# Context products with V as the stationary operand, context laid out channels first, expert weights issued later, in a two-layer gated cross-attention kernel

## The chip, the cores and the metric

The kernel runs on one core of one Trainium2 chip. The metric is device time in microseconds (us) of one execution; the time before is the median of three runs.

## The reference

64 batches of 64 rows, 128 channels: x (the query side) and ctx (keys and values) are both [64, 64, 128]. Two layers follow each other, each a gated cross-attention and a gated mixture of experts:

```python
# layer 0 (masked), layer 1 (no mask); H = 16 heads of DK = 8 channels
q = LN(x) @ wq + bq;  k = ctx @ wk + bk;  v = ctx @ wv + bv
scores = where(mask == 0, -1e9, q . k) / sqrt(8)
x = x + tanh(g_xattn[l]) * (softmax(scores) @ v @ wo + bo)
# experts: layer 0 top-1 of 8 (hidden 512, gelu), layer 1 top-2 of 16 with a capacity (hidden 64, silu)
x = x + tanh(g_ffn[l]) * experts_l(LN(x))
```

All of it is float32.

## The kernel before

The 4096 rows are NT = 32 tiles of 128 rows (two batches each), and 8 groups q of Q = 4 tiles (quartets). x stays in SBUF (x_all). Each layer has one `attention` block, in which all engines run at once, and blocks for the experts. In `attention` each engine has a list of steps (function, every, skew): `run` goes through n, and at each n calls, in the list's order, every step whose turn it is; a step with skew s handles tile n - s (or its group, where `every` is 4). So a step with skew -12 works twelve tiles ahead. Each engine executes its instructions in that order, and semaphores tie the engines together.

The path of a tile t of group q, by engine:

- SP (`block.sync`, lines 236 to 250) issues loads, in order, for each q: x(q) (layer 0 only; line 241), ctx(q) (line 244), mask(q) (layer 0; line 247), and at q == 1 the expert weights of the layer (line 250; in layer 0 about 4.6 MB, in layer 1 1.5 MB). x(q) waits for `ln_stats` Q(q-1), ctx(q) for `ctx_turned` q-1, mask(q) for `mask_made` q-1. In layer 1 x is completed by POOL's `fetch` (line 257), an indirect DMA that adds expert outputs into x_all.
- DVE: `stat`, `aggregate` (skew -12, lines 438 to 449) give mean and variance of x; `stat` waits for x(q). `mask` (skew -4, line 461) makes the mask bias. For each tile `maximum` and `subtract` (skew 0, lines 404 to 419) take the row maxima of the two halves of heads and subtract them. `divide` (every 2 tiles, skew 3, line 421) takes reciprocals of the denominators and multiplies. `add` (skew 6) adds the attention output to x, `r_stat`, `r_aggregate` (skew 8) start the second normalization; `choose`, `rows` (skews 18, 19, layer 0) do routing.
- POOL: `norm` (skew -8), `add_bias` (-4), `blocks` (skew -2, line 284), which spreads k into k_blk by heads, `r_norm` (12), the indirect DMAs, and at the start `clear` (line 261), which zeroes v_blk and writes its columns of ones.
- ACT: `normed` (-8) writes the normalized x, and copies PE's results out of PSUM: `ctxT_out`, `xnT_out`, `q_out`, `k_out`, `v_out`, `exp` (which makes probT, keys on partitions), `avT_out`, and `scale_out` (skew 4, layer 0), which scales the expert weights.
- PE: `turn_ctx` (skew -6, line 516) transposes ctx, since rows arrive on partitions; `turn_x` (-5), `project_q` (-4), `project_k` (-3), `project_v` (-2 and -1), `score` (-1, line 574), `turn_probs` (0), `attend` (1, line 603), `turn_av` (3, line 614), `output` (6, line 621), `turn_r`, `logit`, `rank` for routing.

`score` of the next tile needs both `subtract` of this one (`shifted`), since there is one pair of score buffers. In `attend` the probabilities are the stationary operand and V, with a column of ones per head, moves through; rows come out on partitions, 18 columns per pair of heads:

```python
for j in range(HP):
    for b in range(2):
        last = nc.tensor.matmul(AV[b * S:(b + 1) * S, t % 2 * HP + j, :], probT[:, t % 2, j, b * S:(b + 1) * S],
                                v_blk[:, q % 2, u, b, j, :], start=True, stop=True, skip_group_check=True)
```

So the result has to be transposed (`turn_av`, then ACT's `avT_out`) before `output`.

Of the kernel before, what the change touches and what calls it, by code (L numbers as in the profile page):

```python
# [108 lines left out]
def attention(nc, layer, x_all, w, dram, r, hook, sems):  # L109
# [4 lines left out]
    with ExitStack() as ctx:  # L114
# [14 lines left out]
        ctx_in = sb("ctx_in", [P, 2, Q, D])  # L129
# [38 lines left out]
        AV = A_ps[:, 0:2 * HP * VW].rearrange("p (m c) -> p m c", c=VW)  # L168
# [15 lines left out]
        ctx_turned = sem("ctx_turned")  # L184
        ctxT_ready = sem("ctxT_ready")
# [16 lines left out]
        av_turned = sem("av_turned")  # L202
        avT_ready = sem("avT_ready")
# [32 lines left out]
        def _(sp):  # L236
            for q in range(NQ):
# [5 lines left out]
                wait(sp, ctx_turned, q - 1)  # L243
                sp.dma_start(ctx_in[:, q % 2, :, :], dram["ctx"][rows, :].rearrange("(u p) d -> p u d", p=P)).then_inc(ctx_loaded[q % 2], 16)
# [3 lines left out]
                if q == 1:  # L248
                    for to, what, done in hook["experts"]:
                        sp.dma_start(to, what).then_inc(done, 16)  # L250

        @block.gpsimd
        def _(pool):
# [6 lines left out]

            def clear():
                nc.gpsimd.memset(v_blk[:, :, :, :, :, :], 0.0).then_inc(zeroed, 1)
                pool.wait_ge(zeroed, 1)
                for s in range(2):
                    half = slice(s * S, (s + 1) * S)
                    nc.gpsimd.memset(v_blk[half, :, :, :, :, s:s + 1], 1.0).then_inc(zeroed, 1)
                pool.wait_ge(zeroed, 3)
# [45 lines left out]
            if masked:  # L313
                clear()
# [3 lines left out]
            else:  # L318
                for t in range(Q):
                    fetch(t)  # L320
                clear()
                for t in range(Q, 2 * Q):
                    fetch(t)
# [3 lines left out]
        def _(act):  # L327
# [27 lines left out]
            def v_out(h):  # L355
                def step(q):
                    act.wait_ge(v_made, 2 * q + h + 1)
                    act.wait_ge(zeroed, 3)
                    wait(act, av_made, Q * (q - 2) + 2 * h + 2)
                    for s in range(2):  # L360
                        half = slice(s * S, (s + 1) * S)
                        last = nc.scalar.copy(v_blk[half, q % 2, 2 * h:2 * h + 2, :, :, 2 + s * DK:2 + (s + 1) * DK].rearrange("p u b j d -> p (u b j) d"),
                                              V_ps[half, 2 * h:2 * h + 2, :, :, :].rearrange("p u b j d -> p (u b j) d"))
# [33 lines left out]
            steps = [(xnT_out, Q, -4), (r_xnT_out, Q, 17), (ctxT_out, Q, -5), (avT_out, Q, 6), (v_out(0), Q, -1), (v_out(1), Q, 0)]  # L397
# [5 lines left out]
        def _(dve):  # L403
# [17 lines left out]
            def divide(p):  # L421
                dve.wait_ge(av_made, 2 * p + 2)
                nc.vector.reciprocal(rden[:, :, :], AV[:, :, 0:2]).then_inc(rden_ready, 1)
                dve.wait_ge(rden_ready, p + 1)
                wait(dve, av_turned, p - 1)
                h = p % 2
                nc.vector.tensor_tensor(av[:, 2 * h:2 * h + 2, :].rearrange("p u (j r d) -> p (u j) r d", j=HP, r=2),
                                        AV[:, :, 2:].rearrange("p m (r d) -> p m r d", r=2),
                                        rden[:, :, :].unsqueeze(3).to_broadcast([P, 2 * HP, 2, DK]),
# [54 lines left out]
            def rows(q):  # L484
# [7 lines left out]
                for k in range(Q):  # L492
                    if q * Q + k >= RING:
# [4 lines left out]
                     (divide, 2, 3), (add, Q, 6), (stat, 1, -12), (r_stat, 1, 8), (aggregate, 1, -12), (r_aggregate, 1, 8)]  # L498
            if masked:
# [4 lines left out]
        def _(pe):  # L504
            ident = w["ident"]

            def turn_x(q):
                pe.wait_ge(xn_ready, Q * (q + 1))
                pe.wait_ge(ctxT_ready, q + 1)
                if masked:  # L510
                    wait(pe, counted, q - 5)
# [3 lines left out]

            def turn_ctx(q):
                pe.wait_ge(ctx_loaded[q % 2], 16 * (q // 2 + 1))
                wait(pe, xnT_ready, q)
                wait(pe, chosen_ready if masked else logits_read, q - 5)
                for u in range(Q):  # L520
                    last = nc.tensor.transpose(X_ps[:, u, :], ctx_in[:, q % 2, u, :], ident[:, :])
                last.then_inc(ctx_turned, 1)
# [33 lines left out]
            def project_k(q):  # L556
                pe.wait_ge(ctxT_ready, q + 1)
# [45 lines left out]
            def attend(t):  # L603
# [740 lines left out]
```

## Time and profile before

| | |
|---|---|
| median of 3 runs | 700.67 us (699.44 to 700.93) |
| the profiled execution, its own time | 701.08 us |
| its span | 699.3 us |
| mean granted TensorE clock | 0.895 of full |
| PE busy | 545.9 us (78%) |
| DVE, ACT, POOL busy | 411.7, 298.5, 340.6 us |
| L289 POOL, k_blk, 128 times | 139.5 us busy |
| L599 PE, transposes of probabilities | 83.8 us busy |
| L610 PE, `attend`, 2048 records | 72.6 us busy |
| L423 DVE, reciprocals, 32 times | 11.1 us busy |

Layer 0's attention runs from about 10 to 250 us of the span (its last 40 us are the routing's tail), its experts to 352, layer 1's attention from 354 to about 565, the rest to the end. A busy share is an average over these stages, each with its own limit. In a row of the timeline, the number in brackets is the idle time of the engine just before, and behind the arrow what ended it.

### The profile page before, as it was taken

How to read it: one execution, taken by the hardware profiler on the slowest of the kernel's cores; microseconds unless marked ns; L12 is line 12 of the kernel's file. 1: busy time of each engine (PE TensorE's matmuls, PEld its weight loads, DVE VectorE, ACT ScalarE, POOL GpSimd, SP SyncE). 2: the span in 40 equal slices, each digit the busy share in tenths (PEclk: the TensorE clock that was granted, in tenths of full speed). 3: DMA queues.
4: the chain of work that ended last, by engine and by line, in shares of the span. 5: the costliest groups of instructions: out<-in, count | busy, mean ns of one | idle time of the engine just before them, and what ended most of it. 6: DMA issues, size and time to landing. Idle time of an engine off the chain costs nothing. (4 is left out here: it accounts for less than half of the span.)

```text
span 699.3 us, 17278 instructions
## 1 busy us (share of the span) xinstructions
PE 545.9 (78%) x5350; PEld 369.4 (53%) x5351; DVE 411.7 (59%) x1014; ACT 298.5 (43%) x639; POOL 340.6 (49%) x451
## 2 busy tenths in 40 slices
PE   1389999989996408999913689999999744789776
PEld 0145665656665408888801356656666532333665
DVE  3167788888774333444412367877678528831676
ACT  1335666555443103333302455566665421444443
POOL 3355555567544722222268999996664111310221
PEclk9889999999995558999965799999999855999999
DMA  5921101000000121222182111110000000000011
GB/s 159 283 61 40 38 19 40 10 7 11 18 17 15 46 71 51 60 60 61 52 162 31 30 32 32 33 30 3 2 2 2 1 0 0 0 1 0 28 45 49
DMA packets 48478, 28.02 MB, mean 40 GB/s; under 512 B 11936, under 2 KB 45344, under 8 KB 48416
## 3 DMA queue, kind: packets, MB, share of 16 engines
q1 hardware_dynamic: 42064, 22.20, 11.4%
q0 software_dynamic: 5632, 4.20, 3.4%
q10 hardware_dynamic: 720, 0.81, 0.4%
q8 instruction: 38, 0.62, 0.4%
q14 instruction: 24, 0.20, 0.1%
HBM read 19.46 MB, written 7.73 MB: 39 GB/s over the span
## 5 line engine op out<-in xcount | busy, mean ns | idle before, releaser
L289 POOL TENSOR_TENSOR k_blk<-kT,columns 128x512 f32<-128x512 f32 x128 | 139.5, 1176 | 69.1 <-PE S_ps L588 64.1
L408 DVE TENSOR_REDUCE maxes<-S_ps 128x8 f32<-128x512 f32 x128 | 87.6, 684 | 56.2 <-PE S_ps L588 55.9
L371 ACT ACTIVATE probT<-T_ps 128x512 f32<-128x512 f32 x128 | 76.5, 598 | 71.8 <-PE T_ps L599 70.8
L416 DVE TENSOR_TENSOR prob<-S_ps,maxes 128x512 f32<-128x512 f32 x128 | 88.5, 691 | 4.4
L599 PE MATMUL T_ps<-columns,prob 128*128 128x128 f32 x512 | 83.8, 286 | 4.0 <-DVE prob L416 4.0
L599 PEld LDWEIGHTS T_ps<-columns,prob 128*128 128x128 f32 x512 | 55.7, 142 | 57.8 <-issue 50.3
L588 PE MATMUL S_ps<-k_blk,qT 64*64 64x512 f32 x512 | 71.5, 629 | 6.5 <-POOL k_blk L289 6.0
L610 PE MATMUL A_ps<-v_blk,probT 128*64 128x18 f32 x2048 | 72.6, 214 | 0.2
L610 PEld LDWEIGHTS A_ps<-v_blk,probT 128*64 128x64 f32 x2048 | 66.2, 140 | 11.2 <-issue 11.2
L257 POOL DMA_INDIRECT x_all<-expert_out,row_int x32 | 50.7, 1585 | 16.9 <-POOLq L774 10.4
L911 POOL COPY f_w_now<-f_w 128x512 f32 x39 | 24.0, 616 | 71.1 <-PE f_H_ps L950 58.4
L866 DVE TENSOR_TENSOR f_hid<-f_H_ps,f_b 128x512 f32<-128x512 f32 x39 | 27.0, 691 | 40.1 <-PE f_Y_ps L959 31.9
L928 ACT ACTIVATE f_hid<-f_hid 128x512 f32<-128x512 f32 x39 | 24.6, 631 | 52.6 <-DVE f_hid L866 52.6
L332 ACT ACTIVATE xn<-x_all,shift,rstd 128x128 f32<-128x128 f32 x64 | 30.5, 485 | 37.7 <-POOL shift L277 37.6
L444 DVE BATCH_NORM_STATS2 stats<-x_all 128x6 f32<-128x128 f32 x64 | 18.4, 288 | 46.3 <-DMA x_all<-expert_out,row_int 26.8
L950 PE MATMUL f_H_ps<-f_rowsT,f_w_now 128*128 128x128 f32 x312 | 44.7, 288 | 0.7
L1066 POOL COPY c_slots_now<-outT 128x256 f32 (+1 forms) x32 | 13.3, 418 | 63.8 <-POOLq L972 32.8
L959 PE MATMUL f_Y_ps<-f_w,f_hid 128*128 x312 | 42.9, 281 | 0.6 <-ACT f_hid L928 0.4
L950 PEld LDWEIGHTS f_H_ps<-f_rowsT,f_w_now 128*128 128x128 f32 x312 | 39.6, 199 | 4.5 <-issue 4.2
L959 PEld LDWEIGHTS f_Y_ps<-f_w,f_hid 128*128 128x128 f32 x312 | 37.9, 191 | 3.7 <-issue 3.6
L309 POOL DMA_INDIRECT sorted_rows<-r_xn,r_row x32 | 32.0, 1000 | 9.6 <-issue 9.0
L766 PE MATMUL a_X_ps<-a_dispatch,a_xn_now 128*128 128x256 f32 x64 | 24.1, 473 | 11.9 <-DVE a_dispatch L726 11.5
(172 smaller groups left out, 969.4 us busy)
## 6 DMA issues: line engine op xcount, KB each, us to landing
ctx_in<-in_ctx SPq DMA_DIRECT2D x16, 256.0 KB, 3.1
f_rows<-sorted_rows SPq DMA_DIRECT2D x39, 64.0 KB, 1.8
expert_out<-f_done SPq DMA_DIRECT2D x39, 64.0 KB, 1.6
x_all<-in_x SPq DMA_DIRECT2D x8, 256.0 KB, 3.4
f_w<-in_W SPq DMA_DIRECT2D x1, 2048.0 KB, 9.4
out<-c_final SPq DMA_DIRECT2D x32, 64.0 KB, 1.5
mask_in<-in_mask SPq DMA_DIRECT2D x8, 128.0 KB, 2.3
columns<-in_columns ACTq DMA_DIRECT2D x1, 530.0 KB, 5.1
```

The costliest lines, as they stand in the source:

```text
L257: pool.indirect_dma_start(x_all[:, t * D:(t + 1) * D], None, r["expert_out"], bass.IndirectOffsetOnAxis(ap=r["row_int"][:, t:t + 1], axis= ...
L289: last = nc.gpsimd.tensor_tensor(k_blk[:, t % 2, b, :, :], kT[:, q % 2, u, b * S:(b + 1) * S].unsqueeze(1).to_broadcast([P, HP, S]), w["he ...
L309: pool.indirect_dma_start(r["sorted"], bass.IndirectOffsetOnAxis(ap=row[:, t % RING:t % RING + 1], axis=0), r_xn[:, t % RING, :], None).th ...
L332: nc.scalar.activation(xn[:, u, :], x_all[:, t * D:(t + 1) * D], ACT.Identity, bias=shift[:, q % 2, u:u + 1], scale=rstd[:, q % 2, u:u + 1 ...
L371: nc.scalar.activation(probT[:, t % 2, 4 * g:4 * g + 4, :], T_ps[g][:, :, :], ACT.Exp, scale=SCALE).then_inc(probT_ready, 1)
L408: nc.vector.tensor_reduce(maxes[:, t % 2, heads], S_ps[g][:, :, :], X, ALU.max).then_inc(max_ready, 1)
L416: nc.vector.tensor_tensor(prob[:, t % 2, heads, :], S_ps[g][:, :, :], maxes[:, t % 2, heads].unsqueeze(2).to_broadcast([P, HP, S]), ALU.su ...
L588: last = nc.tensor.matmul(S_ps[g][b * S:(b + 1) * S, :, :], qT[rows, q % 2, u, b * S:(b + 1) * S], k_blk[rows, t % 2, b, :, :], start=not ...
L599: last = nc.tensor.transpose(T_ps[g][:, j, :], pair, ident[:, :])
L610: last = nc.tensor.matmul(AV[b * S:(b + 1) * S, t % 2 * HP + j, :], probT[:, t % 2, j, b * S:(b + 1) * S], v_blk[:, q % 2, u, b, j, :], st ...
L950: last = nc.tensor.matmul(H_ps[T.par][:, n, :], w1_now[:, T.par, n * P:(n + 1) * P], rowsT[:, T.par, :], start=True, stop=True)
L959: last = nc.tensor.matmul(Y_ps[T.par][:, 0:D], hid[:, T.par, n, :], w2[:, bass.ds(e, 1), n, :].rearrange("p a c -> p (a c)"), start=n == 0 ...
```

## The change

- ctx is handed over transposed (`ctxT`, channels first) and loaded straight into the ctxT tile. PE's `turn_ctx` and ACT's `ctxT_out` are gone; the load of ctx(q) now waits until V of group q-2 is made, because it writes into the tile that this product reads.
- `attend` has V as the stationary operand, in pieces of 128x32 (four places side by side), and the probabilities move: 16 products with 64 columns, whose results have channels on partitions; and 8 products of 128x32 blocks of ones with 128 columns, which give the denominators, repeated for every channel. `turn_av` and `avT_out` are gone; avT now has two buffers.
- `divide` takes the reciprocal of 256 denominators per partition (before 32) and writes avT.
- v_blk is wider (32 columns per pair), zeroed by DVE at the start of its queue and no longer by POOL.
- The expert weights are issued at q == 3, behind mask(3), instead of q == 1; `scale_out` has skew 16 instead of 4.

```diff
-VW = 2 + 2 * DK
+VW = 4 * DK
...
-                wait(sp, ctx_turned, q - 1)
-                sp.dma_start(ctx_in[:, q % 2, :, :], dram["ctx"][rows, :].rearrange("(u p) d -> p u d", p=P)).then_inc(ctx_loaded[q % 2], 16)
+                wait(sp, v_made, 2 * (q - 1))
+                sp.dma_start(ctxT[:, q % 2, :, :], dram["ctxT"][:, rows].rearrange("d (u p) -> d u p", p=P)).then_inc(ctx_loaded[q % 2], 16)
...
-                if q == 1:
+                if q == 3:
                     for to, what, done in hook["experts"]:
...
             else:
-                for t in range(Q):
-                    fetch(t)
-                clear()
-                for t in range(Q, 2 * Q):
+                for t in range(2 * Q):
                     fetch(t)
...
-            def ctxT_out(q):
-                act.wait_ge(ctx_turned, q + 1)
-                wait(act, v_made, 2 * (q - 1))
-                nc.scalar.copy(ctxT[:, q % 2, :, :], X_ps[:, :, :]).then_inc(ctxT_ready, 1)
...
-            def avT_out(q):
-                act.wait_ge(av_turned, 2 * q + 2)
-                wait(act, y_made, q)
-                nc.scalar.copy(avT[:, :, :], Y_ps[:, :, :]).then_inc(avT_ready, 1)
...
             def divide(p):
+                q, h = p // 2, p % 2
                 dve.wait_ge(av_made, 2 * p + 2)
-                nc.vector.reciprocal(rden[:, :, :], AV[:, :, 0:2]).then_inc(rden_ready, 1)
+                nc.vector.reciprocal(rden[:, :], DEN).then_inc(rden_ready, 1)
                 dve.wait_ge(rden_ready, p + 1)
-                wait(dve, av_turned, p - 1)
-                h = p % 2
-                nc.vector.tensor_tensor(av[:, 2 * h:2 * h + 2, :].rearrange("p u (j r d) -> p (u j) r d", j=HP, r=2),
...
+                wait(dve, y_made, q - 1)
+                nc.vector.tensor_tensor(avT[:, q % 2, 2 * h:2 * h + 2, :].rearrange("p u c -> p (u c)"), AV, rden[:, :],
                                         ALU.mult).then_inc(divided, 1)
...
+            nc.vector.memset(v_blk[:, :, :, :, :, :], 0.0).then_inc(zeroed, 1)
+            nc.vector.memset(ones_blk[:, :], 0.0).then_inc(zeroed, 1)
...
-                for j in range(HP):
-                    for b in range(2):
-                        last = nc.tensor.matmul(AV[b * S:(b + 1) * S, t % 2 * HP + j, :], probT[:, t % 2, j, b * S:(b + 1) * S],
-                                                v_blk[:, q % 2, u, b, j, :], start=True, stop=True, skip_group_check=True)
...
+                for r in range(2):
+                    for j in range(r, HP, 2):
+                        nc.tensor.matmul(DEN[quarter(j), at:at + P], ones_blk[:, (1 - r) * 2 * DK:(3 - r) * 2 * DK], probT[:, t % 2, j, :],
+                                         start=r == 0, stop=r == 1, skip_group_check=True)
+                for b in range(2):
+                    for r in range(2):
+                        for j in range(r, HP, 2):
+                            from_ = v_blk[:, q % 2, u, b, :, :].rearrange("p j c -> p (j c)")[:, j * VW - r * 2 * DK:(j + 1) * VW - r * 2 * DK]
+                            last = nc.tensor.matmul(AV[quarter(j), at + b * S:at + (b + 1) * S], from_, probT[:, t % 2, j, b * S:(b + 1) * S],
+                                                    start=r == 0, stop=r == 1, skip_group_check=True)
...
             def output(q):
-                pe.wait_ge(avT_ready, q + 1)
+                pe.wait_ge(divided, 2 * q + 2)
+                wait(pe, y_added, q)
...
-            attention(nc, 0, x_all, w0, d, r0, {"experts": experts, "act": [(scale_out, 1, 4)]}, sems)
+            attention(nc, 0, x_all, w0, d, r0, {"experts": experts, "act": [(scale_out, 1, 16)]}, sems)
```

How it moves instructions. SP's queue in layer 0 from the second x load on; f_w and f_b are the expert weights and biases. Before:

```order
L241 DMA x_all<-in_x 128x4x128
L244 DMA ctx_in<-in_ctx 128x4x128
L247 DMA mask_in<-in_mask 128x4x64
L250 DMA f_w<-in_W 128x8x512
L250 DMA f_b<-in_b 128x32
L250 DMA f_b<-in_b 128x1024
L250 DMA f_w<-in_W 128x32x128
L241 DMA x_all<-in_x 128x4x128 [waits ln_stats]
L244 DMA ctx_in<-in_ctx 128x4x128 [waits ctx_turned]
L247 DMA mask_in<-in_mask 128x4x64 [waits mask_made]
```

And now, from the fourth ctx load on:

```order
L239 DMA ctxT<-in_ctxT 128x512 [waits v_made]
L242 DMA mask_in<-in_mask 128x4x64 [waits mask_made]
L245 DMA f_w<-in_W 128x8x512
L245 DMA f_b<-in_b 128x32
L245 DMA f_b<-in_b 128x1024
L245 DMA f_w<-in_W 128x32x128
L236 DMA x_all<-in_x 128x4x128 [waits ln_stats]
L239 DMA ctxT<-in_ctxT 128x512 [waits v_made]
```

The four weight loads moved from ahead of x(2) to ahead of x(4), and every ctx load, with mask and the next x behind it, waits for a V product.

PE's queue at the end of a quartet, from `attend` of the tile to the next scores. Before:

```order
L610 MATMUL A_ps<-v_blk,probT 64x18 [waits probT_ready,divided,v_ready]
L610 MATMUL A_ps<-v_blk,probT 64x18 x15
L513 MATMUL X_ps<-columns,xn 128x128 [waits ctxT_ready,xn_ready]
L513 MATMUL X_ps<-columns,xn 128x128 x3
L618 MATMUL Y_ps<-columns,av 128x128 [waits y_added,divided]
L618 MATMUL Y_ps<-columns,av 128x128
L569 MATMUL Q_ps<-columns,ctxT 64x64 [waits v_ready,kT_ready]
L569 MATMUL Q_ps<-columns,ctxT 64x64 x7
```

And now:

```order
L581 MATMUL A_ps<-probT,ones_blk 32x128 [waits probT_ready,zeroed,divided,v_ready]
L581 MATMUL A_ps<-probT,ones_blk 32x128 x7
L587 MATMUL A_ps<-probT,v_blk 32x64 x16
L487 MATMUL X_ps<-columns,xn 128x128 [waits xn_ready]
L487 MATMUL X_ps<-columns,xn 128x128 x3
L534 MATMUL Q_ps<-columns,ctxT 64x64 [waits v_ready,kT_ready]
L534 MATMUL Q_ps<-columns,ctxT 64x64 x7
```

`attend` has 24 products for 16, and the transposes of av between those of x and the V product are gone.

## Rows read from the trace of the kernel before

**Rows 1.** The page, part 2: granted TensorE clock in 40 slices of the span, in tenths.

```profile
PEclk9889999999995558999965799999999855999999
```

**Rows 2.** Busy time by stretch (layer 0, layer 1), columns engine busy (instructions), clock, DMA share, GB/s.

```profile
80.00:100.00 20.00, 19.40 (x244) 11.90 (x240) 16.28 (x40) 12.14 (x24) 9.66 (x12) 1.00 0.12 34
440.00:460.00 20.00, 18.91 (x256) 12.16 (x248) 15.09 (x38) 11.05 (x23) 19.03 (x23) 1.00 0.16 29
```

**Rows 3.** DVE's timeline, layer 0: start us, us, instruction, idle before and releaser.

```profile
79.12 0.69 DVE L408 TENSOR_REDUCE maxes<-S_ps 128x8 f32<-128x512 f32 x1 [0.99 <-PE S_ps L588]
...
81.77 0.28 DVE L444 BATCH_NORM_STATS2 stats<-x_all 128x6 f32<-128x128 f32 x1
...
82.38 1.00 DVE L464 TENSOR_SCALAR mask_zero<-mask_in 128x256 f32<-128x256 int32 x1
...
84.08 0.42 DVE L468 TENSOR_TENSOR mask_bias<-mask_zero,mask_value 128x256 bf16<-128x256 f32 x1
85.67 0.69 DVE L408 TENSOR_REDUCE maxes<-S_ps 128x8 f32<-128x512 f32 x1 [1.17 <-PE S_ps L588]
...
88.32 0.35 DVE L423 RECIPROCAL rden<-A_ps 128x32 f32<-128x32 f32 x1
...
89.05 0.28 DVE L444 BATCH_NORM_STATS2 stats<-x_all 128x6 f32<-128x128 f32 x1
...
90.34 0.69 DVE L408 TENSOR_REDUCE maxes<-S_ps 128x8 f32<-128x512 f32 x1 [0.60 <-PE S_ps L588]
...
95.63 0.69 DVE L408 TENSOR_REDUCE maxes<-S_ps 128x8 f32<-128x512 f32 x1 [0.18 <-PE S_ps L588]
...
100.50 0.69 DVE L408 TENSOR_REDUCE maxes<-S_ps 128x8 f32<-128x512 f32 x1 [0.80 <-PE S_ps L588]
```

**Rows 4.** DVE's timeline, layer 0, once routing runs beside the attention.

```profile
141.16 0.68 DVE L408 TENSOR_REDUCE maxes<-S_ps 128x8 f32<-128x512 f32 x1
...
145.92 0.68 DVE L408 TENSOR_REDUCE maxes<-S_ps 128x8 f32<-128x512 f32 x1
```

**Rows 5.** Groups of DVE instructions: count, then busy us, mean ns, idle before.

```profile
L423 DVE RECIPROCAL rden<-A_ps 128x32 f32<-128x32 f32 x32 | 11.1, 348 | 5.6 <-PE A_ps L610 5.6
...
L490 DVE TENSOR_TENSOR r_picked<-r_place,r_chosen 128x32 f32<-128x32 f32 x8 | 1.5, 194 | 0.0
```

**Rows 6.** PE's timeline around tile 4 of layer 0.

```profile
57.60 0.66 PE L599 MATMUL T_ps<-columns,prob 128*128 128x128 f32 x4
58.19 1.11 PE L610 MATMUL A_ps<-v_blk,probT 128*64 128x18 f32 x32
...
60.04 0.69 PE L569 MATMUL Q_ps<-columns,ctxT 128*64 128x64 f32 x16
```

**Rows 7.** A group of PE's matmuls, 80 to 120 us.

```profile
L588 PE MATMUL S_ps<-k_blk,qT 64*64 64x512 f32 x56 | 7.6, 614 | 0.0
```

**Rows 8.** SP's timeline of DMA issues, layer 0.

```profile
13.10 0.51 SPq L250 DMA_DIRECT2D f_w<-in_W  x1
...
18.07 10.23 SPq L241 DMA_DIRECT2D x_all<-in_x  x1
...
63.56 0.52 SPq L241 DMA_DIRECT2D x_all<-in_x  x1
```

**Rows 9.** All engines' timeline, start of layer 0.

```profile
26.80 4.05 POOL L289 TENSOR_TENSOR k_blk<-kT,columns 128x512 f32<-128x512 f32 x4 [4.91 <-ACT kT L353]
...
32.97 0.30 DVE L444 BATCH_NORM_STATS2 stats<-x_all 128x6 f32<-128x128 f32 x1 [14.17 <-DMA x_all<-in_x]
...
34.92 1.01 PE L582 MATMUL S_ps<-mask_bias,ident_bf 128*128 128x512 bf16 x2 [7.45 <-DVE mask_bias L468]
```

**Rows 10.** The eight x loads of line 241.

```profile
DMA to landing us min/median/max: 2.8/3.4/14.9
```

**Rows 11.** POOL in the timeline at the start of layer 1.

```profile
361.27 2.64 POOL L262 MEMSET v_blk<- 128x2304 f32 x1
...
363.96 0.71 POOL L266 MEMSET v_blk<- 64x128 f32 x2
```

More of the change, by code:

```diff
@@ L259, in fetch @@
                                         compute_op=ALU.add).then_inc(fetched[t % 4], 16)
[L261 to L267, printed above, removed]
             def norm(q):
@@ L361, in step @@
                         half = slice(s * S, (s + 1) * S)
-                        last = nc.scalar.copy(v_blk[half, q % 2, 2 * h:2 * h + 2, :, :, 2 + s * DK:2 + (s + 1) * DK].rearrange("p u b j d -> p (u b j) d"),
+                        last = nc.scalar.copy(v_blk[half, q % 2, 2 * h:2 * h + 2, :, :, s * DK:(s + 1) * DK].rearrange("p u b j d -> p (u b j) d"),
                                               V_ps[half, 2 * h:2 * h + 2, :, :, :].rearrange("p u b j d -> p (u b j) d"))
@@ L498, in _ @@
                      (divide, 2, 3), (add, Q, 6), (stat, 1, -12), (r_stat, 1, 8), (aggregate, 1, -12), (r_aggregate, 1, 8)]
+            nc.vector.memset(v_blk[:, :, :, :, :, :], 0.0).then_inc(zeroed, 1)
+            nc.vector.memset(ones_blk[:, :], 0.0).then_inc(zeroed, 1)
+            dve.wait_ge(zeroed, 2)
+            for s in range(2):
+                nc.vector.memset(ones_blk[s * S:(s + 1) * S, (2 + s) * DK:(3 + s) * DK], 1.0).then_inc(zeroed, 1)
             if masked:
@@ L514, in turn_x @@
                 last.then_inc(x_turned, 1)
[L516 to L522, printed above, removed]
             def turn_r(q):
@@ L607, in attend, with quarter @@
                 pe.wait_ge(probT_ready, 2 * t + 2)
-                for j in range(HP):
-                    for b in range(2):
-                        last = nc.tensor.matmul(AV[b * S:(b + 1) * S, t % 2 * HP + j, :], probT[:, t % 2, j, b * S:(b + 1) * S],
-                                                v_blk[:, q % 2, u, b, j, :], start=True, stop=True, skip_group_check=True)
-                last.then_inc(av_made, 1)
-            def turn_av(p):
-                pe.wait_ge(divided, p + 1)
-                wait(pe, y_added, p // 2)
-                for u in (p % 2 * 2, p % 2 * 2 + 1):
-                    last = nc.tensor.transpose(Y_ps[:, u, :], av[:, u, :], ident[:, :])
-                last.then_inc(av_turned, 1)
+                pe.wait_ge(zeroed, 4)
+                at = t % 2 * P
+                def quarter(j):
+                    return slice(j // 2 * VW, (j // 2 + 1) * VW)
+                for r in range(2):
[8 more added lines that the diff above has]
+                                                    start=r == 0, stop=r == 1, skip_group_check=True)
+                last.then_inc(av_made, 1)
             def output(q):
-                pe.wait_ge(avT_ready, q + 1)
+                pe.wait_ge(divided, 2 * q + 2)
+                wait(pe, y_added, q)
                 for u in range(Q):
-                    last = nc.tensor.matmul(Y_ps[:, u, :], avT[:, u, :], w["wo"][:, :], start=True, stop=True)
+                    last = nc.tensor.matmul(Y_ps[:, u, :], avT[:, q % 2, u, :], w["wo"][:, :], start=True, stop=True)
                 last.then_inc(y_made, 1)
@@ L629, in _ @@
                 steps += [(rank, Q, 19)]
-            run(steps + [(score, 1, -1), (turn_probs(1), 1, 0), (attend, 1, 1), (turn_ctx, Q, -6), (turn_x, Q, -5), (turn_av, 2, 3),
+            run(steps + [(score, 1, -1), (turn_probs(1), 1, 0), (attend, 1, 1), (turn_x, Q, -5),
                          (turn_r, Q, 16), (logit, Q, 17), (project_v(0), Q, -2), (project_v(1), Q, -1)])
@@ L1299 @@
     arrays = {
-        "x": i["x"].reshape(T, D), "ctx": i["ctx_1024"].reshape(T, D), "mask": i["mask_BxSxS2_ik1"].reshape(T, S),
+        "x": i["x"].reshape(T, D), "ctxT": i["ctx_1024"].reshape(T, D).T, "mask": i["mask_BxSxS2_ik1"].reshape(T, S),
     }
```

27 lines of the change are left out of this document (8 added, 19 removed).

## The prediction

> **What bounds it now.** I read the clock by slice first, then busy time by stretch, then DVE's and PE's timelines for one quartet (four tiles, a group q), then SP's queue, because the change moves a wait there. The clock [rows 1] shows 2.4 GHz (a 9) wherever attention runs and 1.2 GHz (a 5) at its start, before it and after it. By stretch [rows 2], PE is busy 19.40 of 20 us in layer 0 and 18.91 in layer 1, where POOL has 19.03: PE sets the pace in layer 0, PE and POOL together in the first half of layer 1 (`fetch` beside `blocks`). DVE has 16.28 and 15.09, so it has about 4 us per 20 in hand.
>
> DVE's timeline [rows 3] gives the pace: the first score reduction of a tile starts at 79.12, 85.67, 90.34, 95.63, 100.50. A quartet takes 21.38 us, as 6.55 + 4.67 + 5.29 + 4.87, and each start waited for PE (brackets). Inside it, the two maxima and two subtractions take 2.65 us (79.12 to 81.77), the normalization statistics 0.61 (81.77 to 82.38), the mask group 2.1 (to 84.50); a `divide` takes 0.73 (88.32 to 89.05), in every second tile. A tile's chain is: scores, 2.65 us of DVE, next scores. DVE's steps behind those 2.65 us are free as long as they fit under the next scores. Once routing runs, one tile of four has no slack: 141.16 to 145.92 without an idle bracket [rows 4].
>
> **The change, part by part.**
>
> *PE in `attend`.* Now 32 records (each f32 matmul leaves two) fill 1.11 us [rows 6]. After: 16 records with 128 columns and 32 with 64. Score products of 512 columns show the rate: eight records, four side by side, in two rounds; 7.6 us for 56 is 1.09 us per eight, less 0.614 for one is 0.48 per round [rows 7], so at most 0.12 for 128 columns, 0.06 for 64. With four column groups side by side each group runs 4 x 0.12 + 8 x 0.06 = 0.96 us. I cost `attend` at no change. Nothing in the trace has four column groups; the other bound is one after the other, 3.8 us.
>
> *PE and ACT copies removed.* Per quartet four ctx transposes (0.59, as the four from 57.60 to 58.19 [rows 6]) and four av transposes in two pairs (about 0.6), so PE's 21.4 falls to 20.2. The two ACT copies lie beside other work.
>
> *DVE's `divide`.* The reciprocal goes from 32 elements per partition to 256. With 32 it takes 348 ns, an ordinary operation on 32 takes 194 [rows 5]. Bounds: the extra is fixed per instruction, then about 0.6 us for 256; or everything scales, 8 x 0.348 = 2.8. I take the ordinary fixed part and let the rest grow: 194 less about 33 for its elements is 0.16 fixed; 0.19 for 32 is 5.9 ns each; 256 give 1.68 us, +1.33 per `divide`. The nearest row is a reciprocal that is already far slower than its element count. A `divide` tile then needs 2.65 + 0.73 + 1.33 + 0.61 = 5.3 us on DVE. Two of the four, 4.67 and 4.87, become 5.3 (+1.1); the others lose PE work and backlog (5.29 to about 4.4, 6.55 to 6.3). First half of layer 0: about zero. Second half: the tile without slack, 4.76, becomes 6.1, and I count +1.3 per quartet, **+5** in four. In layer 1 POOL holds the first half at 19 of 20 us, and the two gains meet the two losses: **-1**.
>
> The Trainium skill (VectorE: DVE Perf Modes, section First, the fixed hardware budget) says that a reciprocal is an iterative divide with a repeat count of 8. An estimate from that page, eight cycles an element at its 0.96 GHz, is 2.1 us for 256 plus some 0.1; the sum would be up to 16 higher. The trace has one size only and fits either.
>
> *SP's queue: ctx.* `ctx(q)` now waits for `v_made` 2(q-1), the V product of group q-2, where it waited for a transpose five steps earlier. SP is in order, so mask(q) and **x(q+1)** stand behind it. V of q-2 is made at the end of PE's step n = 4q-9; DVE needs x(q+1) at step 4q-8, right behind that tile's four score operations. Before, x(5) was issued at 63.56 [rows 8] for a use at 81.77 [rows 3]. After: V runs from 2.4 us after the scores of its tile and takes 0.69 (60.04 against 57.60 [rows 6]); without av transposes and with `attend` already begun I put its end 2.4 us behind DVE's first reduction. Issues of ctx and mask take 0.9, landing 3.4 (median, [rows 10]) to 5 with those two ahead: x lands 6.7 to 8.3 behind, DVE wants it 2.65 behind. Stall about 4.5; the tile takes 2.65 + 4.5 + 0.6 + 2.1 to 3.0 (mask) = about 10.2 against 6.55. For x(5), x(6), x(7): **+11**.
>
> *SP's queue: experts.* Now the 4.6 MB are issued at 13.10, ahead of x(2), which lands at 32.97: 19.9 us later, 14.17 of it a DVE wait [rows 8, 9]. After, they stand behind mask(3) and ahead of x(4). SP gets there when V of group 1 is made, 2.4 + 0.9 us into tile 4; x(4) lands some 19 us behind that (less is ahead of it than before), 22.2 us into the tile, and `stat(16)` wants it at 2.65. DVE stands 19.5 us, and with it everything. The tile takes 2.65 + 19.5 + 0.6 + 2.1 = 24.9 against 6.55: **+18**. PE's clock falls to 1.2 GHz in such a gap, as in the fives of [rows 1]; at the start it took some 5 us of dense work at half speed to return: **+2.5**.
>
> *Start of layer 0.* The first scores waited 7.45 us for a mask that stood behind x(2); k_blk had been begun at 26.80 [rows 9]. Without that wait, and with DVE first clearing v_blk (4096 elements; POOL's 2304 took 2.64 [rows 11]; I take 4 us, which delays statistics by some 1.5), scores come 4.5 earlier. But x(3) now waits for V of group 0 and lands about where it was used before, so the 4.5 goes back: **0**, and with PE idle in between the clock stays low longer, **+1.5**.
>
> *Start of layer 1.* POOL loses 2.64 + 2 x 0.36 of memsets ahead of its norm and blocks [rows 11], which lead to the first scores: **-3.6**. DVE's memset there lies in a wait for x. *Ends of the layers:* transposes and a copy go, the longer reciprocal comes: **-1**.
>
> Sum: 5 - 1 + 11 + 18 + 2.5 + 1.5 + 0 - 3.6 - 1 = +32.4. The profiled execution took 701.08, the median is 700.67: 733.5, or **733** against the median. About 0.2% is what a measurement can tell from no change.
>
> **Rivals.**
> 1. *x is not late* (faster). If the x loads land in time after all, because transfers behind the experts overtake them or V is made much earlier than I place it, the terms 11, 18, 2.5 and 1.5 go and the start keeps its 4.5: 701.1 + 5 - 1 - 4.5 - 3.6 - 1 = 696. It decides once all x waits of layer 0 together are under 5 us. Against it: x(2) behind the same transfers waited 14.17 us. Chance 0.10.
> 2. *Four column groups do not run side by side.* With pairs, as `attend` runs now, the phase takes 2 x 0.96 = 1.9, +0.9 per tile; PE's quartets become 23.8 and 22.4, above DVE's, some +25 in all: 758; one after the other, +2.8 per tile, over 850. The products on 64x64 pieces do run four at a time, though on two row halves. Chance 0.08. The Trainium skill (TensorE: Matmul & The Clock Gate, Measured speedup vs the span model) has 2.38 for three column tiles. An estimate by that share makes the phase 1.2 us and adds under 15 in all; no run here shows it.
> 3. *The reciprocal is short* (0.6 us): `divide` tiles go back to PE's pace, some 14 less: 719. Chance 0.15.
> 4. *The reciprocal is long* (2.8 us): +1.1 for 32 of them, minus what stalls hide, about +30: 763. Chance 0.07.
>
> **Numbers.** The forecast has 0.60; its own range, from a DMA landing 3 us sooner or later and three stalls of 2 to 6 us, is 722 to 747. 708 to 760 leaves out rival 1, the deeper half of rival 2 and half of rival 4, together under 0.2. Faster 0.10 (rival 1), same 0.02, slower 0.88.
>
> **What would show it.** DVE's statistics should wait for x_all some 19 us once near 60 us and about 4.5 us three times (near 100, 120, 140), no wait of 14 us at the start, SP's experts issued near 62 us, a reciprocal of 1.7 us, `attend` near 1.0 us, first scores of layer 1 3 to 4 us sooner after its barrier. The prediction is wrong if no DVE wait on x_all exceeds 5 us, or if `attend` takes over 1.5 us.

## The result, and the profile after

The changed kernel takes 735.89 us (median, 734.41 to 740.64) against 700.8 for the one before: a ratio of 1.0528 (95% interval 1.0477 to 1.0578). The profiled execution spans 733.1 us against 699.3, 33.8 more. The forecast was 733.

The page of the changed kernel: the clock by slice; then groups of instructions (count, then busy us, mean ns of one, idle time before it and what ended it).

```profile
PEclk9989599998999955799995599999999965899999
...
L397 DVE RECIPROCAL rden<-A_ps 128x256 f32<-128x256 f32 x32 | 55.9, 1747 | 3.0 <-PE A_ps L587 3.0
L415 DVE BATCH_NORM_STATS2 stats<-x_all 128x6 f32<-128x128 f32 x64 | 18.4, 288 | 54.5 <-DMA x_all<-in_x 37.5
...
L581 PE MATMUL A_ps<-probT,ones_blk 128*32 128x128 f32 x1024 | 41.9, 281 | 6.3 <-issue 6.3
...
L587 PE MATMUL A_ps<-probT,v_blk 128*32 128x64 f32 x2048 | 43.3, 222 | 0.7 <-issue 0.7
```

Against [rows 1] a 5 has come into the first quarter (the fifth slice, 73 to 92 us). The reciprocal takes 1747 ns where it took 348 [rows 5]. And DVE waits 37.5 us for x, in six places, where the kernel before waits 18.6 us in three, the 14.17 of [rows 9] among them.

DVE's timeline of the changed kernel, from tile 4 of layer 0, the first of its quartet, to tile 9:

```profile
59.37 0.66 DVE L381 TENSOR_REDUCE maxes<-S_ps 128x8 f32<-128x512 f32 x1
...
82.29 0.30 DVE L415 BATCH_NORM_STATS2 stats<-x_all 128x6 f32<-128x128 f32 x1 [20.21 <-DMA x_all<-in_x]
84.02 0.68 DVE L381 TENSOR_REDUCE maxes<-S_ps 128x8 f32<-128x512 f32 x1
...
86.67 1.75 DVE L397 RECIPROCAL rden<-A_ps 128x256 f32<-128x256 f32 x1
...
90.81 0.69 DVE L381 TENSOR_REDUCE maxes<-S_ps 128x8 f32<-128x512 f32 x1 [1.52 <-PE S_ps L553]
...
95.49 0.69 DVE L381 TENSOR_REDUCE maxes<-S_ps 128x8 f32<-128x512 f32 x1 [0.51 <-PE S_ps L553]
...
100.68 0.66 DVE L381 TENSOR_REDUCE maxes<-S_ps 128x8 f32<-128x512 f32 x1
...
107.43 0.29 DVE L415 BATCH_NORM_STATS2 stats<-x_all 128x6 f32<-128x128 f32 x1 [4.05 <-DMA x_all<-in_x]
...
109.81 0.68 DVE L381 TENSOR_REDUCE maxes<-S_ps 128x8 f32<-128x512 f32 x1
```

This is the same view as [rows 3], where a quartet's first reductions stood 6.55, 4.67, 5.29 and 4.87 apart. Here the tile that begins at 59.37 takes 24.65 us, with 20.21 of it a wait for x(4). The next takes 6.79. From 100.68 to 109.81 a quartet's first tile takes 9.13, with 4.05 of it a wait for x(5).

SP's timeline of the changed kernel (start us, us):

```profile
61.63 0.34 SPq L239 DMA_DIRECT2D ctxT<-in_ctxT  x1
62.02 0.43 SPq L242 DMA_DIRECT2D mask_in<-in_mask  x1
62.50 0.51 SPq L245 DMA_DIRECT2D f_w<-in_W  x1
...
64.31 0.86 SPq L245 DMA_DIRECT2D f_w<-in_W  x1
65.21 12.82 SPq L236 DMA_DIRECT2D x_all<-in_x  x1
102.95 0.33 SPq L239 DMA_DIRECT2D ctxT<-in_ctxT  x1
103.33 0.43 SPq L242 DMA_DIRECT2D mask_in<-in_mask  x1
103.80 0.51 SPq L236 DMA_DIRECT2D x_all<-in_x  x1
```

The V product lets the ctx load go 2.26 us behind the tile's first reduction (61.63 against 59.37), the experts go next, and x(4) is issued at 65.21 and used at 82.29: 17.1 us. The issue alone held SP for 12.82, where x(2) behind the same loads took 10.23 [rows 8]. For x(5): released 2.27 behind the reduction (102.95 against 100.68), issued at 103.80, used at 107.43, which is 6.75 behind. The eight x loads together:

```profile
DMA to landing us min/median/max: 2.7/3.6/17.1
```

To see where the 33.8 us come from I cut both profiled spans at the first reduction of a tile (`maximum(0)`) and list each piece beside the recorded terms:

| piece, us | before | after | difference | recorded |
|---|---|---|---|---|
| start to the first reduction of layer 0 | 37.92 | 33.46 | -4.5 | -4.5 |
| tiles 0 to 3 (x(3)) | 19.82 | 25.91 | +6.1 | +4.5 and +1.5 |
| tile 4 (x(4), experts) | 6.55 | 24.65 | +18.1 | +18 |
| the tile behind it (slow clock) | 4.67 | 6.79 | +2.1 | +2.5 |
| tiles 8, 12, 16 (x(5) to x(7)) | 19.65 | 28.41 | +8.8 | +11 |
| rest of layer 0 | 118.6 | 125.5 | +6.9 | +5 |
| last reduction of layer 0 to first of layer 1 | 185.18 | 179.19 | -6.0 | -3.6 and part of -1 |
| layer 1, first reduction to last | 151.99 | 152.64 | +0.7 | -1 |
| from there to the end of the span | 154.9 | 156.6 | +1.6 | part of -1 |

The sum is 33.8. Layer 0 alone holds +42 from its first to its last reduction.

PE's timeline of the changed kernel, one `attend` in layer 0:

```profile
169.06 0.64 PE L581 MATMUL A_ps<-probT,ones_blk 128*32 128x128 f32 x16
169.52 0.63 PE L587 MATMUL A_ps<-probT,v_blk 128*32 128x64 f32 x32
170.08 1.06 PE L504 MATMUL X_ps<-columns,r_xnT 128*128 128x8 f32 x8
```

From its start to that of the next matmuls, 169.06 to 170.08, are 1.02 us. In the kernel before the same stretch for its 32 records (58.19 in [rows 6], to the line below) is 1.04:

```profile
59.23 0.66 PE L513 MATMUL X_ps<-columns,xn 128*128 128x128 f32 x4
```

### The profile page after: what moved, and what is told of

Its sections match the earlier page's. It is cut to its first block and busy times, and to the rows that moved or that the text cites. A ratio compares the mean times of both kernels' runs of the same rounds, so it can differ in the third digit from the quotient of the medians.

```text
span 733.1 us, 19016 instructions
## 1 busy us (share of the span) xinstructions
PE 537.1 (73%) x6246; PEld 351.6 (48%) x6247; DVE 457.7 (62%) x1022; ACT 280.9 (38%) x607; POOL 335.4 (46%) x445
## 5 line engine op out<-in xcount | busy, mean ns | idle before, releaser
L564 PE MATMUL T_ps<-columns,prob 128*128 128x128 f32 x512 | 86.2, 291 | 41.2 <-DVE prob L389 41.0
L553 PE MATMUL S_ps<-k_blk,qT 64*64 64x512 f32 x512 | 75.4, 661 | 8.4 <-POOL k_blk L276 6.4
L397 DVE RECIPROCAL rden<-A_ps 128x256 f32<-128x256 f32 x32 | 55.9, 1747 | 3.0 <-PE A_ps L587 3.0
L415 DVE BATCH_NORM_STATS2 stats<-x_all 128x6 f32<-128x128 f32 x64 | 18.4, 288 | 54.5 <-DMA x_all<-in_x 37.5
L581 PE MATMUL A_ps<-probT,ones_blk 128*32 128x128 f32 x1024 | 41.9, 281 | 6.3 <-issue 6.3
L587 PE MATMUL A_ps<-probT,v_blk 128*32 128x64 f32 x2048 | 43.3, 222 | 0.7 <-issue 0.7
L587 PEld LDWEIGHTS A_ps<-probT,v_blk 128*32 128x32 f32 x2048 | 39.0, 112 | 1.5 <-issue 1.2
```

Of the source, the lines that this page charges most:

```text
L397: nc.vector.reciprocal(rden[:, :], DEN).then_inc(rden_ready, 1)
L553: last = nc.tensor.matmul(S_ps[g][b * S:(b + 1) * S, :, :], qT[rows, q % 2, u, b * S:(b + 1) * S], k_blk[rows, t % 2, b, :, :], start=not ...
L564: last = nc.tensor.transpose(T_ps[g][:, j, :], pair, ident[:, :])
L581: nc.tensor.matmul(DEN[quarter(j), at:at + P], ones_blk[:, (1 - r) * 2 * DK:(3 - r) * 2 * DK], probT[:, t % 2, j, :], start=r == 0, stop=r ...
L587: last = nc.tensor.matmul(AV[quarter(j), at + b * S:at + (b + 1) * S], from_, probT[:, t % 2, j, b * S:(b + 1) * S], start=r == 0, stop=r ...
```

## The experiments

Three things were to be told apart: what the order of SP's loads costs, what the reciprocal costs, and what the new form of `attend` itself is worth. Kernels of one series ran on one chip: runs 1 to 4, then 5, 6, 8 and 9, then 7 and 10. The kernel before had medians of 698.56, 697.16 and 700.31 in the three, and each ratio is against the kernel before on the same chip.

**1. x issued ahead of ctx.** `x_ahead` is the changed kernel with one edit on SP: x(0) and x(1) first, then x(q+1) ahead of ctx(q) and thus ahead of its wait for a V product.

```
-                if masked:
-                    wait(sp, ln_stats, Q * (q - 1))
-                    sp.dma_start(x_all[... q ...]).then_inc(x_in[q % 2], 16)
+                for n in (([0, 1] if q == 0 else [q + 1] if q + 1 < NQ else []) if masked else []):
+                    wait(sp, ln_stats, Q * (n - 1))
+                    sp.dma_start(x_all[... n ...]).then_inc(x_in[n % 2], 16)
```

> The changed kernel, with one thing moved: SP issues x(q+1) ahead of ctx(q) instead of behind mask(q), so no x load stands behind a wait for a V product, and x(4) stands ahead of the expert weights. Theory (the loss is late x loads): the DVE waits on x_all of 3.7, 20.2 and three times 3.4 to 5.4 us go, with the slow clock behind them; 736 falls by some 35 (18.1 + 2.1 for x(4), 8.8 for x(5) to x(7), some 6 at the start) to about 701, between 696 and 706. Rival (the longer reciprocal or the wider attend holds the pace, the waits only show it): it stays above 725.

Measured: 697.83 us, ratio 0.997 (0.9936 to 1.0004). The waits of DVE in this kernel, 9 to 160 us (in total, times, longest):

```profile
DVE maxes L381 <- PE S_ps L553: 15.1, 8, 9.9
...
DVE stats L415 <- DMA x_all<-in_x: 0.3, 1, 0.3
```

Of the 37.5 us of waits for x 0.3 are left, by three lines of SP's program, and with the waits the whole loss is gone. Layer 0 from first to last reduction takes 170.59 us for 211.24 in the changed kernel. Tile by tile, the 40.7 us between them lie in the tiles with a wait for x(3) to x(7) and in the one or two right behind each; every other tile takes the same in both kernels within 0.06 us. x(4) now goes out ahead of ctx(3) and of the experts, and the load behind the experts is x(5), wanted only a quartet later. In the profile of run 8, the same kernel, SP's timeline reads:

```profile
35.53 0.51 SPq L236 DMA_DIRECT2D x_all<-in_x  x1
55.28 0.34 SPq L239 DMA_DIRECT2D ctxT<-in_ctxT  x1
...
58.30 1.26 SPq L245 DMA_DIRECT2D f_w<-in_W  x1
59.60 12.13 SPq L236 DMA_DIRECT2D x_all<-in_x  x1
```

x(4) leaves at 35.53 for 65.21. What the change lost, it lost in the queue that loads x.

**2. Only the experts back.** `experts_back` is the changed kernel with the expert loads ahead of x(2) again.

```
-                if q == 3:
+                if q == 1:
...
-            attention(nc, 0, ..., {"experts": experts, "act": [(scale_out, 1, 16)]}, sems)
+            attention(nc, 0, ..., {"experts": experts, "act": [(scale_out, 1, 4)]}, sems)
```

> The changed kernel with the expert weights issued at q == 1 again (and scale_out at skew 4). Theory: the wait of 20 us at tile 4 becomes one of 3 to 5 like the others, the 14 us wait for x(2) at the start returns: 736 - 20 + 3 + 4.5 is about 723. Rival (the place of the weights does not matter, only the wait for V does): 736.

Measured: 723.85 us, ratio 1.0343 (1.0288 to 1.0397). DVE's timeline of this kernel, its waits for x:

```profile
32.60 0.29 DVE L415 BATCH_NORM_STATS2 stats<-x_all 128x6 f32<-128x128 f32 x1 [13.11 <-DMA x_all<-in_x]
44.08 0.30 DVE L415 BATCH_NORM_STATS2 stats<-x_all 128x6 f32<-128x128 f32 x1 [3.80 <-DMA x_all<-in_x]
70.09 0.30 DVE L415 BATCH_NORM_STATS2 stats<-x_all 128x6 f32<-128x128 f32 x1 [3.91 <-DMA x_all<-in_x]
...
147.03 0.29 DVE L415 BATCH_NORM_STATS2 stats<-x_all 128x6 f32<-128x128 f32 x1 [3.87 <-DMA x_all<-in_x]
```

The 20.21 has become an ordinary wait of 3.91, and 13.11 is back at the start, where attention had not begun. The five waits that are left, 3.80 to 4.06 us each, come from ctx's wait for V alone. So the place of the experts is worth 12 us of the loss (735.89 against 723.85; 13 by the two ratios). The kernel is still 26 us above `x_ahead` (697.83). In the profiled executions ctx's wait accounts for 22 us of that, in layer 0 (192.67 from first to last reduction for 170.59). Another 4 lie before the first reduction (37.54 for 33.42) and belong to the early experts, with their wait of 13.11; the 6.5 between the layers lie for the most part in a stretch that varies (run 10).

**3. The experts late in the kernel before.** `before_experts_late` makes the opposite edit in the kernel before (`q == 3`, `scale_out` at 16), and nothing else.

> The kernel before with only the weights moved to q == 3 (and scale_out at skew 16). Theory: late weights are harmless by themselves, because there SP reaches them at about 39 us and x(4) lands near 58, when it is wanted near 56; the wait of 14 us for x(2) goes and the first scores come about 6 us sooner: 695 to 699. Rival (weights ahead of x(4) cost 18 us wherever SP stands): about 713.

Measured: 697.06 us, ratio 0.9966 (0.9934 to 0.9998). The waits of DVE in this kernel, 9 to 160 us:

```profile
DVE stats L444 <- DMA x_all<-in_x: 7.5, 3, 3.5
```

Without ctx's wait for V, late experts do not hurt: x(4) is issued early enough behind them (at 40.92) that DVE waits 3.46 us there. Layer 0 is 4.8 us longer for it (174.11 for 169.27 from first to last reduction), and the start gains more (the first reduction is at 30.87 for 37.92). So late experts alone cost nothing (-0.3%), the change with early experts, whose loss is the wait for V, costs 3.4% (run 2), and both 5.3%: the same edit is harmless in one kernel and costs 12 us in the other. The experts put some 17 us between issue and landing, and the wait for V puts the issue at the moment of use.

**4. The old `attend` with everything else.** `rows_attend_x_ahead` is `x_ahead` with the products, the reciprocal over 32 elements, the two transposes and the copy of the kernel before, but ctx still loaded channels first. Its diff is the part of the recorded diff on `attend`, `divide`, `turn_av` and `avT_out`, reversed, with GpSimd's `clear` back.

> The kernel before with ctx loaded channels first (no turn_ctx, no ctxT_out), x(q+1) issued ahead of ctx(q), weights at q == 3; attend, divide, turn_av and avT_out as before. Theory (the wide reciprocal takes back what attend's new layout frees, the rest of the change is a gain): 6 us sooner at the start, about 0.5 us of PE per quartet in layer 0 and the second half of layer 1: 688 to 695, below x_ahead. Rival (the new attend is itself a gain): x_ahead is below this one.

Measured: 692.83 us, ratio 0.9928 (0.9895 to 0.9962), 5 us under `x_ahead`. Of the layers the gain is in layer 1: 149.4 us from first to last reduction against 152.7 in `x_ahead`. The first reduction of layer 0 is 1.8 us sooner (31.65 for 33.42), without VectorE's clear of v_blk ahead of the statistics.

**5. A cheap instruction for the reciprocal.** `x_ahead_copy` measures what the long reciprocal costs on the path; it leaves out the division.

```
-                nc.vector.reciprocal(rden[:, :], DEN).then_inc(rden_ready, 1)
+                nc.vector.tensor_copy(rden[:, :], DEN).then_inc(rden_ready, 1)
```

> x_ahead with a plain copy of the 256 denominators where the reciprocal stands, so the attention is multiplied by its denominators, not divided: division is left out. Theory (the 1.75 us reciprocal sets the tiles with a divide, 5.2 to 5.4 us): the copy takes about 0.42, those tiles fall to 4.1 to 4.7 us, 32 of them less what PE then needs: 12 to 20 us below x_ahead, about 682. Rival (PE's wider attend, not the reciprocal, holds those tiles): within 3 us of x_ahead.

Measured: 677.91 us, ratio 0.9729 (0.9693 to 0.9765); 12.6 us under `x_ahead` on the same chip (690.54, run 8). A group of DVE's instructions in this kernel:

```profile
L397 DVE COPY rden<-A_ps 128x256 f32<-128x256 f32 x32 | 13.3, 415 | 1.6 <-PE A_ps L587 1.6
```

DVE is busy 32 x 1.33 = 42.6 us less, and the kernel is 12.6 us shorter. From first to last reduction layer 0 gets 2.8 us shorter (165.98 for 168.81) and layer 1 5.0 (146.75 for 151.78); the stretches behind the layers have 3.2 and 1.9. Most of the 3.2 is in the stretch that varies by 6 us (run 10), so 7.8 us, 18% of the 42.6, are sure to be the reciprocal's, and 12.6, or 30%, only if that stretch is too. The chain that decides is what the prediction said of a `divide` tile: in run 8 such tiles take 5.2 to 5.4 us, here mostly 4.7 in layer 0 and 4.0 to 4.1 in the first half of layer 1. Part of that goes back in the tiles ahead: the first of a quartet in layer 0 takes 6.29 us where it took 5.78 (tile 4).

**6. Column groups one behind the other.** `x_ahead_grouped` changes only the order of the products in `attend`, so that all of one 32-column group stand together.

```
-                for r in range(2):
-                    for j in range(r, HP, 2):
+                for i in range(0, HP, 2):
+                    for r, j in ((0, i), (1, i + 1)):
                         nc.tensor.matmul(DEN[...], ...)
-                for b in range(2):
-                    for r in range(2):
-                        for j in range(r, HP, 2):
+                for i in range(0, HP, 2):
+                    for b in range(2):
+                        for r, j in ((0, i), (1, i + 1)):
                             last = nc.tensor.matmul(AV[...], ...)
```

> x_ahead with the same 24 products in attend in another order: all products of one column group of 32 before the next, instead of the four groups in turn. Theory A (each column group has a queue of its own and runs as soon as its operands are free, whatever the order): attend stays near 1.0 us, time as x_ahead. Theory B (products start in program order, so only neighbours that differ in their column group run side by side): attend takes 2.5 us or more, PE sets the pace of every tile, 750 or above.

Measured: 714.16 us, ratio 1.0255 (1.0218 to 1.0292). Neither theory. PE's timeline of this kernel:

```profile
445.71 0.67 PE L581 MATMUL A_ps<-probT,ones_blk 128*32 128x128 f32 x16
446.17 1.37 PE L587 MATMUL A_ps<-probT,v_blk 128*32 128x64 f32 x32
447.47 0.66 PE L564 MATMUL T_ps<-columns,prob 128*128 128x128 f32 x4
```

The products with ones, four records in a row for each group, take what they took, but the AV products, eight in a row, take 1.37 us for 0.63. `attend` is 1.76 us long (445.71 to 447.47), and the kernel 23.6 us longer than `x_ahead` on the same chip. So the four groups do run side by side in the order of `x_ahead`, and an order in the program can take that away.

**7. Four records in a row for AV.** `x_ahead_grouped_av4` leaves the products with ones as in `x_ahead` and puts `for i` inside `for b`, so that four AV records of a group stand in a row.

```
                 for b in range(2):
-                    for r in range(2):
-                        for j in range(r, HP, 2):
+                    for i in range(0, HP, 2):
+                        for r, j in ((0, i), (1, i + 1)):
```

> x_ahead with only the AV products reordered: one column group's two products (four records) one behind the other before the next group's, for each half of the tile; the products with ones stay as in x_ahead. In x_ahead_grouped four records in a row left the products with ones as they were (0.67 us) and eight in a row made the AV products 1.37 us instead of 0.63. If what decides is how many records of one group stand in a row, the AV products here take 0.63 to 0.75 us and the time equals x_ahead (690 to 698 us, -1 to 0%). If what decides is the number of columns between two groups or something in the AV products themselves, they take 1.0 us or more and the time is 12 us or more above it.

Measured: 698.43 us, ratio 0.9977 (0.9946 to 1.0007), as `x_ahead`. PE's timeline of this kernel:

```profile
454.32 0.64 PE L581 MATMUL A_ps<-probT,ones_blk 128*32 128x128 f32 x16
454.78 0.68 PE L587 MATMUL A_ps<-probT,v_blk 128*32 128x64 f32 x32
455.39 0.66 PE L564 MATMUL T_ps<-columns,prob 128*128 128x128 f32 x4
```

Four in a row cost almost nothing (0.68 us), eight double the phase. Eight records of 64 columns and four of 128 are the same number of columns, and only the first is slow. That points to the number of records in a row and not of columns. It isn't shown for both kinds of products: eight in a row were tried for the AV products alone. What in TensorE sets that number stays open.

**8. `x_ahead` again.** The same kernel as in run 1, on the chip of runs 5, 6 and 9.

> x_ahead once more, on the chip of these runs, for the comparison with its two variants and with the kernel before: 0.3% below the kernel before, as in the first series, interval from -0.6% to 0.

Measured: 690.54 us (688.92 to 691.43), ratio 0.9915 (0.9886 to 0.9944), outside what was expected. Why is open. Cut as in the table of the result, the profiled execution of run 1 is longer by 1.8 us in layer 0, 0.9 in layer 1 and 1.3 behind it, and shorter by 1.2 between the layers.

**9. Layer 1's clear on VectorE, old `attend`.** `rows_attend_clear_dve` is run 4 with GpSimd's clear of v_blk in layer 1 moved to VectorE.

```
             def clear():
+                if not masked:
+                    return
...
+            else:
+                nc.vector.memset(v_blk[:, :, :, :, :, :], 0.0).then_inc(zeroed, 1)
+                dve.wait_ge(zeroed, 1)
+                for s in range(2):
+                    nc.vector.memset(v_blk[s * S:(s + 1) * S, :, :, :, :, s:s + 1], 1.0).then_inc(zeroed, 1)
```

> rows_attend_x_ahead with v_blk of layer 1 cleared by DVE instead of POOL, ahead of DVE's first wait for x (layer 0 as it was). Theory: POOL loses 3.4 us of memsets ahead of its norm and blocks, which lead to the first scores of layer 1, and DVE's memsets lie in its wait for x: 3 to 4 us below rows_attend_x_ahead, about 689. Rival (the first scores wait for the indirect fetches anyway): no difference.

Measured: 687.88 us (687.04 to 689.34), ratio 0.9886 (0.9858 to 0.9915): under both kernels, and under `x_ahead` on the same chip (690.54) by 0.4%, though the two intervals overlap. Against `x_ahead_again` the profiled execution is 1.8 us sooner at the first reduction and 3.3 shorter in layer 1 (148.53 for 151.78), as in run 4. Against run 4, on another chip, the ratio is 0.4% lower, some 3 us, as expected; the table of run 10 has 2.8 of them behind the first gather. It takes from the change ctx loaded channels first, late experts and no clear on GpSimd in layer 1, and leaves out the new `attend`.

**10. That clear alone, in the kernel before.** `before_clear_dve` makes the edit of run 9 in the kernel before.

> The kernel before with one edit: in layer 1 VectorE clears v_blk and sets its ones at its start, instead of GpSimd between its first four gathers and the next. My recorded term for the start of layer 1 is -3.6 us. If it holds, the first score reduction of layer 1 comes 3 to 4 us sooner after the last of layer 0 (185.2 us in the kernel before) and the time is 0.4 to 0.6% lower. The rival reads the -6.0 us between the layers as the end of layer 0 (no transposes and no copy of av, one wait less) and the gathers as limited by something else: then the interval stays at 184 to 185.2 us and the time within 0.3% of the kernel before.

Measured: 698.13 us, ratio 0.9964 (0.993 to 0.9998). From the last reduction of layer 0 to the first of layer 1 it takes 183.95 us for 185.18. That is just under what the rival allowed, the ratio lies between the two expectations, and it would seem to refute the term of -3.6. Cut into its stretches it does not. Ends of the stretches: the first matmul of the experts' hidden layer, the first gather of `fetch`, the first `norm` of layer 1, the first reduction.

| profiled span, us | last reduction to experts | experts to gather | gather to norm | norm to scores |
|---|---|---|---|---|
| before | 58.12 | 89.34 | 17.47 | 20.25 |
| `before_clear_dve` | 58.88 | 90.09 | 14.14 | 20.84 |
| changed kernel | 54.29 | 89.99 | 14.06 | 20.85 |
| `x_ahead` | 54.82 | 89.40 | 14.05 | 20.87 |
| `x_ahead_again` | 55.73 | 89.76 | 14.05 | 20.84 |
| `x_ahead_grouped_av4` | 60.49 | 90.30 | 14.06 | 20.84 |
| `rows_attend_x_ahead` | 54.10 | 90.27 | 17.47 | 20.26 |
| `rows_attend_clear_dve` | 57.68 | 89.45 | 14.05 | 20.84 |

The third and fourth columns repeat to 0.1 us and depend on the clear alone: -3.4 and +0.6, or -2.8 net. The first column spreads over 6 us between kernels whose programs are alike there: runs 4 and 9 have the same layer 0, and 54.10 and 57.68. So a difference of a few us in it can't be put down to an edit. What makes it vary is open, and so is why 0.6 us come back between the norm and the scores.

## Why the prediction was right

By its own steps:

- *The experts, +18.* The tile took 24.65 us against 24.9 forecast and 6.55 before: +18.1. The release came 2.26 us behind the reduction (2.4 forecast), and x(4) was used 22.9 us behind it (82.29 less 59.37, for 22.2). DVE waited 20.21 where I had 19.5, and the statistics and the mask behind it took 1.73 us for 2.7, so two small errors offset each other. The wait of x(2) at the start [rows 9] was the right row to price it by. Run 2 takes this wait away by moving the experts, and run 3 shows that it needs ctx's wait as well.
- *x(5) to x(7), +11: the term was too large.* It measured +8.8. The waits are 4.05, 5.35 and 3.89, or 4.43 on average, for 4.5 forecast: the three were used 6.75, 8.06 and 6.60 us behind the reduction, for 6.7 to 8.3 in that step, and x(6) alone took near 5 us from issue to use (128.70 to 133.83). What was too large is what follows the wait, statistics and mask, with 1.94 to 2.68 us where I had 2.7 to 3.6.
- *Slow clock, +2.5.* The tile behind the gap took 6.79 us for 4.67, +2.1; in `x_ahead` it takes 5.20, so 0.5 of that is the reciprocal and 1.6 the clock. Busy time by stretch of the changed kernel (columns as in [rows 2]) shows the gap and what followed:

```profile
62.00:82.00 20.00, 4.34 (x66) 2.05 (x64) 0.08 (x1) 2.64 (x6) 4.61 (x5) 0.69 0.89 271
84.00:92.00 8.00, 6.52 (x58) 3.03 (x62) 6.30 (x11) 2.26 (x4) 1.08 (x2) 0.61 0.00 0
109.00:116.00 7.00, 4.73 (x20) 2.18 (x20) 6.39 (x14) 1.67 (x3) 0.19 (x1) 0.76 0.01 4
135.00:143.00 8.00, 5.76 (x50) 2.32 (x54) 7.11 (x15) 2.58 (x5) 0.97 (x1) 0.79 0.00 0
161.00:170.00 9.00, 7.28 (x68) 3.44 (x68) 7.22 (x14) 3.26 (x6) 1.51 (x2) 0.62 0.00 2
```

  In the gap PE is busy 4.34 of 20 us, while the DMA engines are at 0.89 with the experts; in the 8 us behind it the mean granted clock is 0.61, so mostly the 1.2 GHz level. The last three rows, behind the waits for x(5) to x(7), have 0.76, 0.79 and 0.62; there I had put nothing for the clock.
- *Start of layer 0, 0 and +1.5.* First reduction 4.46 sooner, the next quartet 6.1 longer, so +1.6. DVE's clear delayed k_blk by 1.5 (28.31 against 26.80 [rows 9]), as put; it took 3.47 us where I had 4. The wait for x(3) was 3.67.
- *The reciprocal, 1.68 us.* Measured 1.747. Two sizes now give the slope: (1747 - 348) / 224 = 6.2 ns an element, and 0.15 us fixed, for 5.9 and 0.16 in that step. The Trainium skill's repeat count of 8 (VectorE: DVE Perf Modes, section First, the fixed hardware budget) had given an estimate of 2.1 us and some 0.1; the trace disagrees, by 0.4 to 0.5 us. Rivals 3 and 4, the short and the long reciprocal, fall with the same row. Rival 3's gain of 14 was well sized if all of run 5's 12.6 for a copy of 0.415 us is the reciprocal's.
- *Rest of layer 0, +5: a size too large and a term left out.* It measured +6.9. `x_ahead`, which has the reciprocal and no waits, is only 3.0 us above the kernel before in the same tiles: three tiles without slack cost 1.3 to 1.4 us each, where I counted four, and in the first half gains and losses nearly meet. The other 3.9 us are in the one or two tiles right behind the waits for x(5) to x(7), where the rows above have the slow clock. I had that cost for the gap of x(4) alone.
- *`attend`, no change.* 0.96 us forecast, 1.02 measured. Rival 2 falls in this program order. The Trainium skill's 2.38 for three column tiles (TensorE: Matmul & The Clock Gate, section Measured speedup vs the span model) gave 1.2 us by an estimate; four groups here come nearer to full overlap. Run 6 shows that rival 2's price was real, one reordering away: +0.74 us per `attend` and +23.6 us, where I had put +0.9 and some +25.
- *Start of layer 1, -3.6: mis-sized.* The table gives -2.8 here and -2.7 in run 10. GpSimd did lose its 3.4 us, but 0.6 comes back between the norm and the scores.
- *Layer 1, -1.* Measured +0.7. The two gains did not meet the two losses fully, and run 5 shows the reciprocal worth 5.0 us in that layer. The saved transposes and the freed slots hide part of it, not all.
- *Ends, -1.* The last pieces came out at +1.6 in layer 1 and, of the -6.0 between the layers, -3.2 in layer 0. The -3.2 lies in and behind the stretch that varies by 6 us, so this term can't be judged.

The mechanism and the large terms were right. The errors were small and of both signs: -2.2, -0.4, +1.9, +0.8, +1.7, with +0.2 in the start and the x(4) tile and -0.6 in the ends. That they leave only 1.4 of the 33.8 is luck, and the +1.9 is itself 3.9 left out against 2.0 too much. *Rival 1*, x in time, would have been 696. Runs 1 and 8 built it, at 0.997 and 0.9915 of the kernel before, or 698.6 and 694.7 against its 700.67. Its size was right, and a different order of three lines would have made it the result.

## What to carry over

When a load gets a new wait, list what stands behind it in the same queue and when each is wanted. Here the late 4.6 MB alone cost nothing and the wait without them 3.4%, and together they stopped VectorE for 20 us at a stretch. And price the clock behind every stall, not only behind the longest. Put the loads that the critical engine wants first ahead of any load that waits for the engine's own progress. And before you trade a small reciprocal for a large one to save transposes, multiply it out in elements per partition: at 6.2 ns each, 256 are longer than two score reductions, and even with the queue mended the old form came out 0.4% ahead (runs 8 and 9), at the edge of what these runs can tell, with 3.3 us of layer 1 in its favour in both series.

## What was not expected of the hardware

- How far groups of 32 columns overlap depends on how closely their records alternate in the program: 16 records with up to four of one group in a row take 0.64 to 0.67 us, 32 AV records take 0.63 with two in a row, 0.68 with four and 1.37 with eight.
- The reciprocal grows by 6.2 ns an element, against (415 - 194) / 224 = 1.0 ns between an ordinary operation over 32 [rows 5] and the copy over 256.
- An x load issued behind the 4.6 MB of experts holds SP itself: the issue took 12.82 us in the changed kernel, 11.03 in `experts_back` and 12.13 in `x_ahead_again`, against 0.4 to 0.5 elsewhere. Everything behind it in SP's queue waits with it.
- The stretch from the last reduction of layer 0 to the first product of the experts' hidden layer takes 54 to 60 us in different executions of like programs. Between `x_ahead_again` and `x_ahead_grouped_av4` it makes 4.8 of the 7.6 us by which their spans differ.
